# A message-passing layer: three instead of two of its 25 node groups summed from gathered rows of x

## The reference

```python
h = x @ W_node.T + b_node
e = edge_attr @ W_edge.T + b_edge
msg = (h[src] + e) @ W_msg.T + b_msg
s = segment_sum(msg, dst, n)
deg = segment_sum(ones, dst, n)
out = layernorm(x + s / maximum(deg, 1)[:, None], axis=-1, eps=1e-5)
```

## Time and profile before

| what | value |
| --- | --- |
| median of three runs | 785.0 us |
| the profiled execution, its own time | 783.87 us |
| its span (first to last instruction) | 782.0 us |
| TensorE busy | 688.6 us, 88% |
| TensorE weight loads | 620.7 us, 79% |
| VectorE busy | 630.1 us, 81% |
| ScalarE busy | 438.3 us, 56% |
| GpSimd busy | 270.0 us, 35% |
| moved by DMA | 130.71 MB, mean 167 GB/s |

### The profile page before, as it was taken

How to read it: one execution, slowest core, us unless ns; L and a number is a source line. 1 busy time by engine, 2 the same in 40 slices (tenths; PEclk the granted TensorE clock), 3 DMA queues, 4 the chain that set the end, 5 groups by cost and what they waited for, 6 DMA issues and landing times.

```text
span 782.0 us, 24842 instructions
## 1 busy us (share of the span) xinstructions
PE 688.6 (88%) x10360; PEld 620.7 (79%) x10360; DVE 630.1 (81%) x1155; ACT 438.3 (56%) x897; POOL 270.0 (35%) x210
## 2 busy tenths in 40 slices
PE   3265577899999989999999998999999999999995
PEld 3244466778888979989988987988998998989994
DVE  7989896868998878878878877789798788779822
ACT  3322496656565556556556555656665665656641
POOL 2737300301443836426426455532543542000000
PEclk9998698999999999999999999999999999999998
DMA  6953543434556574474472575464574574454000
GB/s 174 321 182 79 138 135 111 167 111 146 183 190 194 187 260 156 160 258 158 159 262 55 184 253 195 152 229 156 194 238 146 192 236 153 173 182 169 17 14 16
DMA packets 81518, 130.71 MB, mean 167 GB/s; under 512 B 12100, under 2 KB 25126, under 8 KB 81303
## 3 DMA queue, kind: packets, MB, share of 16 engines
q1 hardware_dynamic: 73230, 115.79, 44.3%
q0 software_dynamic: 7200, 12.39, 5.7%
q10 hardware_dynamic: 974, 0.90, 0.5%
HBM read 125.80 MB, written 3.23 MB: 165 GB/s over the span
## 4 chain that ended last, share of the span: by engine, by line
PE 52%; DVE 11%; issue 4%; POOL 2%; DMA 1%; DVEq 1%; ACT 0%; POOLq 0%
PE x_ps L745 29%; PE count_ps L730 10%; PE win_ps L666 8%; DVE key_hot L886 3%; DVE row_hot L886 2%; PE win_ps L673 2%; POOL x_gathered L607 2%; DMA x_gathered<-in_x_dram,x_index 1%; PE misc_ps L761 1%; PE misc_ps L762 1%; DVE y L932 1%; DVEq L863 1%; DVE y L925 1%; DVE onehot L852 1%; DVE sums_e L876 1%
## 5 line engine op out<-in xcount | busy, mean ns | idle before, releaser
L1416 ACT CAST region<-count_ps 128x490 bf16<-128x490 f32 x575 | 324.3, 573 | 192.8 <-PE count_ps L730 188.5
L745 PE MATMUL x_ps<-region,x_rest 128*128 128x250 bf16 x2254 | 413.6, 270 | 0.0
L745 PE MATMUL x_ps<-region,x_hi 128*128 128x250 bf16 x1127 | 306.2, 272 | 0.5 <-ACT region L1416 0.5
L607 POOL DMA_INDIRECT x_gathered<-in_x_dram,x_index x144 | 195.1, 1355 | 278.5 <-PE count_ps L730 258.9
L886 DVE TENSOR_TENSOR row_hot<-iota_bf,row 125x3200 bf16<-125x3200 bf16 x115 | 209.4, 1821 | 42.1 <-PE count_ps L730 29.1
L730 PE MATMUL count_ps<-key_hot,row_hot 125*128 125x98 bf16 x2875 | 224.4, 209 | 15.2 <-ACT region L1416 8.6
L745 PEld LDWEIGHTS x_ps<-region,x_rest 128*128 128x128 bf16 x2254 | 211.4, 98 | 16.2
L730 PEld LDWEIGHTS count_ps<-key_hot,row_hot 125*128 125x128 bf16 x2875 | 185.6, 99 | 37.9 <-issue 10.4
L886 DVE TENSOR_TENSOR key_hot<-iota_bf,key 125x2500 bf16<-125x2500 bf16 x115 | 167.2, 1454 | 0.0
L666 PE MATMUL win_ps<-edges,onehot 128*32 128x128 f32 x3232 | 107.2, 286 | 13.7 <-DVE onehot L852 12.1
L745 PEld LDWEIGHTS x_ps<-region,x_hi 128*128 128x128 bf16 x1127 | 109.5, 97 | 8.0 <-ACT region L1416 0.6
(11 more groups left out here) (194 smaller groups left out, 415.7 us busy)
## 6 DMA issues: line engine op xcount, KB each, us to landing
edges<-in_edge_attr_dram SPq DMA_DIRECT2D x101, 1024.0 KB, 5.8
resid<-in_x_dram SPq DMA_DIRECT2D x25, 125.0 KB
out_dram<-y SPq DMA_DIRECT2D x25, 125.0 KB
x_gathered<-in_x_dram,x_index POOLq DMA_INDIRECT x144
region<-in_dst_dram ACTq DMA_DIRECT2D x1, 768.0 KB
win_src<-in_src_dram,clipped_int POOLq DMA_INDIRECT x23, 4.4
x_index<-in_src_dram SPq DMA_DIRECT2D x9, 8.0 KB, 5.7
region<-in_L_gnn_W_node_dram SPq DMA_DIRECT2D x1, 64.0 KB
```

The source lines that it names most:

```text
L607: pool.indirect_dma_start(out=x_gathered[:, i, :], out_offset=None, in_=x[:, :], in_offset=bass.IndirectOffsetOnAxis(ap=x_index[:, k, i:i ...
L745: mm = pe.matmul(x_ps[m % 2][:, 0:NB], rows, counts[m % 2][:, b, :], start=(n == 0), stop=(n == PARTS - 1))
L1416: act.copy(counts[m % 2][:, :, f * FILL * 2:(f + 1) * FILL * 2], count_ps[fill % COUNT_BANKS][:, 0:FILL * KEYS].rearrange("p (n b) -> p b ...
```

## The change

Constants: three groups are gathered, so there are 22 rounds and 13 blocks of gathered rows. The region of `sums_e` in which the x sums of gathered groups are kept grows from 700 to 950 columns.

```diff
-GX = 2
-XBLOCKS = 9
+GX = 3
+XBLOCKS = 13
 X_COLS = 2000
-X_LONG = 700
+X_LONG = 950
...
-    x_round = [5 + 14 * k // (XBLOCKS - 1) for k in range(XBLOCKS)]
+    x_round = [6 + k + (k >= XBLOCKS // 2) for k in range(XBLOCKS)]
...
-    X_DONE = [5, 9]
+    X_DONE = [5, 9, 13]
...
         u = x_slot[X_DONE[i] - 1] + SEGS
-        finishes.append((u if u not in x_slot else u + SEGS, None, i))
+        finishes.append((u if u not in x_slot else u - SEGS + 3, None, i))
...
         room = (x_round[k] - x_round[k - 1] if k > 0 else 2) * ROUND_FILLS
-        x_fill.append([x_round[k] * ROUND_FILLS + XSEG * FILLS - room + 2 + (room - 9) * i // (TILES - 1) for i in range(TILES)])
+        x_fill.append([x_round[k] * ROUND_FILLS + XSEG * FILLS - room + 2 + (room - 6) * i // (TILES - 1) for i in range(TILES)])
...
-                while ts and hot[0] < min(NS, ts[-1] + ONEHOT_SLOTS):
+                while ts and hot[0] < min(NS, ts[-1] + 1 + (ONEHOT_SLOTS if u >= LEAD else ONEHOT_SLOTS - 1)):
                     make_onehot(hot[0])
                     hot[0] += 1
```

## The result

The changed kernel takes **830.67 us**, the median of four runs (829.83 to 834.24). The kernel before, run beside it, takes 784.25 us (783.43 to 785.41). The ratio is 1.060, with a 95% interval of 1.057 to 1.063: 46 us slower. The forecast was 4 us slower, the upper end of the range 803 us.

A forecast was written before the change was run, and what follows sets the result against it. TensorE was taken to bound every round. Terms of -16.1, -15.5, +0.6 and +35.1 us summed to +4.1, giving 789 us against a median of 785.0 (0.5% slower), range 773 to 803 us.

The forecast's parts named there:

- TensorE's work: On TensorE: one round goes (-27.2 us), four edge blocks move to x slots (+10.2), a third gathered finish (+0.9): -16.1 us.
- Gaps that go: On TensorE: one-hot gaps (12.1 us), old row waits (2.3) and one finish wait (1.1) vanish: -15.5 us.
- The start: Slot 2 of round 0: one more one-hot stands ahead of VectorE's weight, which TensorE waits for: +0.6 us.
- The wait for gathered rows: In the 13 x slots: TensorE waits for each block's 16th gather, mean 2.9 us in nine of them: +35.1 us in all.
- I let the 16th gather have the place of the window load: GpSimd's queue, round 6: the 16th gather starts at 274.44 and lands 4.4 us later, so TensorE waits 2.5 us.
- The clock: TensorE's granted clock: it fell with an 8.5 us wait, not a 1.6 us one; no term in the sum.
- rival 2: In x slots: the wait feeds itself; the next 1 MB load starts before the 16th gather lands: 803 us, up to 818; one in six.
- Rival 1: In x slots: the 16th gather lands in 3.4 us, as in a quiet stretch, wait 1.5 us: 771 us; a fourth.
- The rule on packets: DMA queues: engines go round queues packet by packet, so a 64 KB gather would hardly feel the edge loads.
- VectorE beside GpSimd: VectorE's two-port operations lock GpSimd out of writing descriptors; the full rule would add 55 us, given no chance of its own.

The follow-up runs named there:

- the fastest version: Changed kernel with x slots in slot 1, first gather one fill earlier, shorter hold, edge load held until the gathered rows are summed: 761.75 us, ratio 0.970.
- The fillers: 36 idle matmuls before each x slot's wait for rows: on the changed kernel 821.86 us; on the changed kernel with the edge load held, 803.77 us.

## Why the prediction was wrong

- **TensorE's work, -16.1: right.** A round of 27.24 us, and 29.67 us of work in an x round of the fastest version, where the clock held; its total busy time is 673.8 us for the 672.5 of the sum. **Gaps that go, -15.5: right**, by the list of waits. **The start, +0.6: right** (+1.0).
- **The wait for gathered rows: right in place, and in mechanism but for the next load; wrong in size.** I predicted 35.1 us, it was 59.1. The step that failed is "I let the 16th gather have the place of the window load", 2.9 us in an x slot. It took the landing of 4.4 us from a stretch in which the next edge load came after the gather had all but landed, and then, two sentences on, removed the gap that kept that load away. In the five rounds with the load 0.5 us behind the gather the waits were 5.9 to 6.4 us, 31 in sum for the 14.5 that I gave them, and round 11 had 8.6 for 4.0. Those two make 21 of the 24 us. The gathers of the five rounds were not in the window load's place either: they started 6.3 us behind the pair's first load and not 4.8, and landed in 6.1 to 6.7 us and not 4.4. Rounds 7 and 14 to 16, where the load came later, waited 2.3 to 3.4, near the 2.9 that I had put; round 19 waited 3.4 for my 2.4, and the two held blocks 2.0 and 2.65 for my 1.3.
- **The clock: predicted 0 in the sum, measured 22.** I wrote that waits of 3 to 4 us lie between two known cases, and left it in rival 2. The trace had the row against me: the mean wait of 2.9 us that I forecast already stood above the longest wait known to be harmless, 1.6 us. The one fall that I named was read wrongly: the clock was at half from 75.5 us on, and that wait of 8.5 us began only at 78.1. The fillers showed that half of this is a net price, at least in the version with the held load.
- **Rival 2, given one in six, is what happened**, in five of the eleven rounds that it spoke of and not in all: the slot's own next load was issued before the gather had landed and delayed it. Its own upper end (818 us) was still 13 short, because I priced the clock in it at nothing. Two losses that feed on each other are not independent terms: a long wait drops the clock, and the longer work moves the next release.
- **Rival 1**, rows landing as in a quiet stretch, is true in slot 1: 2.5 to 3.1 us there. In slot 3 with a load less than 9 us ahead it is so in seven x slots of all runs (2.8 to 3.4 us), each 5 us or more behind the first load ahead of it and none with a load issued within 1.5 us behind the gather.
- **The rule on packets.** The Trainium skill (DMA: Bandwidth & Descriptors, "Queues, rings and completion order") says that each DMA engine goes round its queues packet by packet. I read it so that a 64 KB gather passes a megabyte almost unhurt. Here the gather's landing is tied to the megabytes ahead of it in every line of the table with a load less than 6 us ahead, and in round 11 above its queue moved nothing for 4.7 us beside SyncE's. Measurement decides against that reading of the rule. How the turns are given, and when the gather's descriptors were ready, no run shows.
- **VectorE beside GpSimd** brought no loss of the full 55 us: a gather's mean duration is 1.28 us with 208 of them, for 1.36 with 144, and GpSimd was busy 41% of the time.

**Left open.** Why the landings of one place still differ by 1 to 2.7 us. Why GpSimd's issues take 25.0 us in one round and 26.3 in the next, which decides who wins the race. Round 11's wait: its round 10 has no pair in slot 4, which brings the x slot closer; putting a pair there was not tried.

## What to carry to other kernels

A gap on the bounding engine can be the spacer that keeps a large transfer behind a small urgent one. Before taking a gap away, list what starts earlier without it, each queue's next issue included, and set those times beside every landing that is still waited for. Keep small gathers on the critical path several microseconds away from megabyte loads, by place first (28 us here) and by holding the load until the small one has landed second (18 us in the changed kernel). And give a wait longer than any that the trace shows to be harmless a price for the clock as well.

## What was not expected of the hardware

- One microsecond of order decides. With a pair's first load 6.3 us ahead, a 1 MB load issued 0.5 us **behind** a 64 KB gather's start delayed it in 12 cases of 12 (rows 12.3 to 13.5 us from that first load), and one issued 1.6 us or more behind did not in 16 of 16 (9.2 to 11.8). The gather's own instruction takes 0.94 to 1.2 us on GpSimd, so what may decide is whether the load is issued before it ends. The 7.08 us of round 11 above fit (load at 1.2 us, instruction 2.18 us long). Against it stand two gathers without a pair ahead that landed after 2.78 and 2.91 us with a load 0.91 us behind, 0.03 us before they ended. No run varied this alone.
- Landing time is not a property of the gather: in one place of the program it took 2.5 us, in another 8.4, and what changed little, while the gather started up to 5.2 us behind it, was the time since the first megabyte ahead of it (7.5 to 10.5 us).
- The granted clock fell to its lower level for 3.4 or 6.8 us at a time (10.2 at the waits of 7.6 and 8.6 us). In the kernels with early one-hots and no filler it fell at every wait for rows over 2.7 us, at none under 1.9 us, and in between at 17 of 24: with the window load last, it fell in rounds 13 and 14 (2.22 us each) and not in 16 (2.30).
- An added wait made the kernel 18 us faster, and a removed one made it 15 us slower.
